# Feed-forward steps placed among attention tiles, in a two-layer audio tower on one core

## The reference

```python
ao = (gelu(concat([x, pp]) @ hop_w1 + hop_b1) @ hop_w2 + hop_b2)   # pp: phases of the positions
center, width = tanh(ao[..., :P]) * PI, sigmoid(ao[..., -1:]) * 2 + 0.1
# queries: cos/sin of center in a window of five, weighed by width; keys: tanh(x @ cpe_w) etc.
gate = sigmoid(gelu(x @ sg_w1) @ sg_w2)
st_ph = tanh(gelu(concat([x, cumsum(x @ kce_w) / pos]) @ ksk_w1) @ ksk_w2) * PI
retrieved = causal linear attention over cos/sin features, position phases and stored keys
h = h + x + layernorm(retrieved) @ out_w + out_b                   # x: layernorm(h)
f = layernorm(h)
rh = relu(f @ router_w1 + router_b1); top two of softmax(rh @ router_w2), their softmax as weights
h = h + sum over the two: w * (relu(relu(f @ w1 + b1) @ w2 + b2) @ w3 + b3)
```

## Time and profile before

| | |
|---|---|
| Three runs | 1338.63, 1339.23, 1341.33 us (median 1339.23) |
| The profiled execution | 1339.48 us, its span 1337.6 us |
| PE busy (share of span) | 1221.2 us (91%) |
| DVE | 776.2 us (58%) |
| ACT | 641.5 us (48%) |
| POOL | 527.1 us (39%) |
| Mean granted clock of PE | 0.912 |

### The profile page before, as it was taken

The page is one execution under the profiler, slowest core; times in us unless marked ns, Lnnn a source line. Parts: engine busy times, 40 slices in busy tenths (PEclk is TensorE's granted clock), DMA queues, the critical chain, the costliest instruction groups (busy, mean ns, idle before and its releaser), DMA issues.

```text
span 1337.6 us, 27027 instructions
## 1 busy us (share of the span) xinstructions
PE 1221.2 (91%) x10203; PEld 789.4 (59%) x10203; DVE 776.2 (58%) x1724; ACT 641.5 (48%) x1372; POOL 527.1 (39%) x1111
## 2 busy tenths in 40 slices
PE   6989999999999999999999997799708889889998
PEld 4755665666666666666666664545305676675553
DVE  3545555655556566565565661143677898985542
ACT  1236555555555554555555553050255664744564
POOL 3111454754554644545455444306871020421200
PEclk9979999999999999999999999799757667568999
DMA  4100000000000000000000001102110000000001
GB/s 84 18 5 2 2 3 2 4 6 2 4 2 2 3 2 2 2 2 2 3 2 3 2 2 32 62 34 48 17 14 1 1 1 1 13 1 0 13 12 23
DMA packets 34076, 14.57 MB, mean 11 GB/s; under 512 B 30738, under 2 KB 31346, under 8 KB 33949
## 3 DMA queue, kind: packets, MB, share of 16 engines
q1 hardware_dynamic: 29341, 10.95, 3.6%
q0 software_dynamic: 4608, 1.91, 1.5%
HBM read 6.46 MB, written 7.27 MB: 10 GB/s over the span
## 4 chain that ended last, share of the span: by engine, by line
PE 70%; DVE 11%; POOL 6%; issue 5%; ACT 4%; SPq 2%; DMA 1%; POOLq 0%; DVEq 0%; ACTq 0%
PE psum L755 20%; PE psum L736 10%; PE psum L664 8%; PE psum L727 7%; PE psum L711 4%; POOL XN L1311 3%; PE psum L1008 2%; PE psum L649 2%; DVE arena L1979 2%; PE psum L988 1%; PE psum L809 1%; PE psum L822 1%; PE psum L1023 1%; PE psum L688 1%; SPq L1094 1%
## 5 line engine op out<-in xcount | busy, mean ns | idle before, releaser
L1429 ACT ACTIVATE arena<-psum 125x500 f32<-125x500 f32 x576 | 307.0, 585 | 329.8 <-PE psum L736 329.8
L1780 DVE TENSOR_REDUCE arena<-psum 125x1 f32<-125x500 f32 x384 | 242.5, 674 | 199.9 <-PE psum L664 199.8
L664 PE MATMUL psum<-arena 32*125 32x500 f32 (+1 forms) x1536 | 322.4, 516 | 0.3 <-ACT arena L1420 0.3
L755 PE MATMUL psum<-arena,XN 125*64 125x250 f32 x2304 | 307.4, 387 | 0.2 <-ACT arena L1429 0.2
L736 PE MATMUL psum<-arena 32*125 32x250 f32 x2304 | 291.7, 370 | 0.0
L736 PEld LDWEIGHTS psum<-arena 32*125 32x125 f32 x2304 | 214.6, 183 | 11.8 <-issue 1.0
L755 PEld LDWEIGHTS psum<-arena,XN 125*64 125x64 f32 x2304 | 140.2, 136 | 121.2 <-issue 78.4
L1783 DVE TENSOR_REDUCE arena<-psum 125x2 f32<-125x500 f32 x192 | 121.3, 674 | 71.1 <-PE psum L664 66.9
L664 PEld LDWEIGHTS psum<-arena 32*125 32x125 f32 x1536 | 126.4, 183 | 3.7 <-DVE arena L1780 1.0
L727 PE MATMUL psum<-arena,onesb 3*125 3x500 bf16 x576 | 122.4, 422 | 2.1 <-DMA arena<-arena 2.1
L1204 POOL TENSOR_TENSOR lnst<-lnst,mhalf 125x12 f32<-125x12 f32 x14 | 32.0, 2286 | 231.3 <-DVE lnst L1759 231.3
(11 more groups left out here) (343 smaller groups left out, 1948.7 us busy)
## 6 DMA issues: line engine op xcount, KB each, us to landing
arena<-arena SPq DMA_DIRECT2D x192, 1.5 KB
expert_in<-XN SPq DMA_DIRECT2D x8, 256.0 KB, 4.8
arena<-expert_in SPq DMA_DIRECT2D x4, 512.0 KB, 5.3
expert_out<-arena SPq DMA_DIRECT2D x4, 512.0 KB, 3.1
out<-H SPq DMA_DIRECT2D x16, 93.8 KB
expert_in<-XN,slot_in POOLq DMA_INDIRECT x48
XN<-expert_out,slot_out POOLq DMA_INDIRECT x48, 3.8
arena<-in_L_ffn_w SPq DMA_DIRECT2D x2, 256.0 KB
```

What stands on the lines that cost most here:

```text
L664: last = pe.matmul(ps[0:R, at_:at_ + hi - lo], QH[row:row + 32, b, g, j * R:(j + 1) * R], KH[row:row + 32, b, g, lo:hi], start=True, stop= ...
L755: last = pe.matmul(ctx_bank[64 * h2:64 * h2 + 64, 0:THIRD], XN[:, p, c, a, :], PR[:, x % 4, h2, i * THIRD:(i + 1) * THIRD], start=(c == 0) ...
L1429: act.activation(PR[:, x % 4, h2, :], st_bank[(2 * x + h2) % 3][0:R, 0:2 * THIRD], ACT.Exp)\
L1780: dve.reduce_max(MX[:, q % 2, 0, 2 * h2 + tile:2 * h2 + tile + 1], ps[0:R, 0:2 * THIRD], AX)\
```

## The change

The list of events is written anew behind tile 7. A chain of 13 events per quarter (norm 2, product, norm 3, router, logit, weighed, gates) runs from x = 6p + 8 on at two events per x: one behind features(x), one behind the next quarters' preparation. Each x from 13 on takes one step, 28 steps in all, without a condition. Within a step the order is turned round: gate_spread of item x - 2 and layer3 come first, then layer1 of x, layer2 of x - 1, and turned a step later than before; DVE gates item x - 2.

To make room for the feed-forward's buffers beside attention's, the features are kept in two copies, HG, KG, SG, CX, RH, GP and YS in one, H2 in 6 parts instead of 12, with waits on the last reader where a copy went; late weights lie in the tiles of layer 0's Q, K and VO. POOL clears these ahead of its events, and the loads on SP follow that.

PPF and DVE's addition go; PE adds a product of the positions' phases (32 rows) to hop's product in PSUM, and ACT's Gelu reads PSUM with the bias.

Behind the list of events, the diff shows in this order: PE's `hidden` and step, POOL behind gather(3) and ahead of its events, ACT's `hidden` and step (`summed` moves ahead of `hidden1`, one step later), DVE's `gated` and step.

```diff
-        HG, at = view(0, [2 * L])
+        HG, at = view(0, [L])
...
-        CV, at = view(at, [3 * NJ, 2, 2, D], parts=R)
+        CV, at = view(at, [2 * NJ, 2, 2, D], parts=R)
...
+        qkf, vof = qkp.rearrange("p a b c -> p (a b c)"), vox.rearrange("p a b -> p (a b)")
+        e1w = qkf[:, 0:384].rearrange("p (a b) -> p a b", a=3)
...
+        H2, at = view(at, [6, HALF])
...
-        ROOM, FIRST, PER = 16, 23, 1
...
+        FIRST = 13
+        chain = [("centre", 2), ("variance", 2), ("normalize", 2), ("transpose", 2), ("product", 0), ("centre", 3),
+                 ("variance", 3), ("normalize", 3), ("transpose", 3), ("router",), ("logit",), ("weighed",), ("gates",)]
+
+        def late(x, slot):
+
+            return [(*chain[n], p) for p in range(NP) for n in (2 * (x - NJ * p - 8) + slot,) if 0 <= n < len(chain)]
+
+        todo = [("step", k) for k in range(len(steps1) + 4)]
...
             if x < NT:
                 events.append(("features", x))
+            events += late(x, 0)
             if x < NT and k in (0, 2):
...
-            if x == ROOM:
-                events.append(("room", 0))
-            for _ in range(PER if x >= FIRST else 0):
-                k = todo[0][1]
-                if x > gate_at[steps1[min(k, len(steps1) - 1)][0]] + 3:
-                    events.append(todo.pop(0))
+            events += late(x, 1)
+            if x >= FIRST and todo:
+                events.append(todo.pop(0))
...
+                        last = pe.matmul(ps[0:w.shape[1], 0:HALF], w, XT[:, cols], start=True, stop=(name == "sg"))
+                        if name == "hop":
+                            last = pe.matmul(ps[:, 0:HALF], W["hop1b"][0:PP, :], ppt[:, th * HALF:(th + 1) * HALF],
+                                             start=False, stop=True)
...
+                    if 2 <= x < len(steps1) + 2:
+                        gate_spread(x - 2)
+                    if x >= 5 and x % 3 == 2:
+                        layer3(x // 3 - 1)
                     if x < len(steps1):
                         layer1(x)
                     if 1 <= x <= len(steps1):
-                        gate_spread(x - 1)
                         layer2(x - 1)
-                    if x >= 4 and x % 3 == 1:
-                        layer3(x // 3 - 1)
-                    if x >= 5 and x % 3 == 2:
-                        turned(x // 3 - 1)
+                    if x >= 6 and x % 3 == 0:
+                        turned(x // 3 - 2)
...
+            pool.memset(b3r, 0.0)
+            pool.memset(e2w, 0.0).then_inc(S["late_zero"], 1)
+            link(pool.memset(GP, 0.0))
...
+            pool.tensor_scalar(SEL.rearrange("r p e d -> r (p e) d"), over(ramp, 6, D), 0.0, None,
+                               ALU.is_equal).then_inc(S["select"], 1)
...
-                    emptied(act, ("hop", p, th))
-                    act.activation(HG[:, own], HG[:, own], ACT.Gelu).then_inc(S["hop_act"], 1)
+                    ps, done = filled(act, ("hop", p, th))
+                    act.activation(HG[:, own], ps[:, 0:HALF], ACT.Gelu, bias=W["hopb"]).then_inc(done, 1)
...
+                    if x >= 5 and x % 3 == 2:
+                        summed(x // 3 - 1)
...
-                    if n >= 2:
-                        i = jobs[("l3", n - 2)]
+                    if n >= 1:
+                        i = jobs[("l3", n - 1)]
                         dve.wait_ge(full[i % 8], i // 8 + 1)
...
-                    if 1 <= x <= len(steps1):
-                        gated(x - 1)
-                    if x >= 5 and x % 3 == 2:
-                        added(x // 3 - 1)
+                    if 2 <= x < len(steps1) + 2:
+                        gated(x - 2)
+                    if x >= 6 and x % 3 == 0:
+                        added(x // 3 - 2)
```

More of the change, by code:

```diff
@@ L139, in build @@
         assert at <= ASIZE - 3 * 768
-        PPF = sb("PPF", [128, L])
+        ppt = sb("ppt", [PP, L])
         QH, at = view(0, [B, 2, L])
@@ L598, in _ @@
                         .then_inc(done, 1)
[L599 to L604, removed]
             for half in range(2):
@@ L866, in tokens @@
                         emptied(pe, ("ksk", p, th))
-                    pe.wait_ge(S["hop_act"], 2 * (p + 1))
+                    for th in range(2):
+                        emptied(pe, ("hop", p, th))
                 for i in range(NJ * p + 3 * h, NJ * p + 3 * h + 3):
                     cols = slice(i * R, (i + 1) * R)
-                    own = slice((i - p // 2 * 2 * NJ) * R, (i - p // 2 * 2 * NJ + 1) * R)
+                    own = slice((i - NJ * p) * R, (i - NJ * p + 1) * R)
                     ps, done = take(pe, ("tok", i))
@@ L898, in masked @@
                 p, j = divmod(x, NJ)
-                g = 2 * NJ * (p % 3) + 2 * j
+                g = 2 * NJ * (p % 2) + 2 * j
                 for k in range(2):
@@ L1326, in _ @@
             gather(3)
+            pool.memset(b3r, 0.0)
+            pool.memset(e2w, 0.0).then_inc(S["late_zero"], 1)
+            link(pool.memset(GP, 0.0))
+            for n in range(4):
+                link(pool.iota(out=ramp[32 * n:32 * n + 32, :], pattern=[[1, 6]], base=0,
+                                 channel_multiplier=-1, allow_small_or_imprecise_dtypes=True))
+            pool.tensor_scalar(SEL.rearrange("r p e d -> r (p e) d"), over(ramp, 6, D), 0.0, None,
+                               ALU.is_equal).then_inc(S["select"], 1)
             for event in events:
@@ L1337, in _ @@
                     scale(x, event[2])
-                elif kind == "room":
-                    k = jobs[("ao", NT - 1)]
-                    pool.wait_ge(full[k % 8], k // 8 + 1)
-                    pool.memset(b3r, 0.0)
-                    pool.memset(e2w, 0.0).then_inc(S["late_zero"], 1)
-                    link(pool.memset(GP, 0.0))
-                    for n in range(4):
-                        link(pool.iota(out=ramp[32 * n:32 * n + 32, :], pattern=[[1, 6]], base=0,
-                                         channel_multiplier=-1, allow_small_or_imprecise_dtypes=True))
-                    pool.tensor_scalar(SEL.rearrange("r p e d -> r (p e) d"), over(ramp, 6, D), 0.0, None,
-                                       ALU.is_equal).then_inc(S["select"], 1)
         @block.scalar
@@ L1381, in _ @@
                     last.then_inc(done, 1)
-                    for h in range(2):
-                        ps, done = filled(act, ("ppf", h))
-                        act.activation(PPF[:, h * HALF:(h + 1) * HALF], ps[:, 0:HALF], ACT.Identity, bias=W["hopb"])\
-                           .then_inc(done, 1)
             act.wait_ge(S["trig_r"], 1)
@@ L1592, in gate_tiles @@
             def gate_tiles(p):
-                if p == 0:
-                    i = jobs[("ret", 3 * NJ - 1)]
-                    act.wait_ge(full[i % 8], i // 8 + 1)
                 for th in range(2):
@@ L1617, in summed @@
                 ps, done = filled(act, ("l3", n))
-                if n >= 2:
-                    k = jobs[("yt", n - 2)]
+                if n >= 1:
+                    k = jobs[("yt", n - 1)]
                     act.wait_ge(full[k % 8], k // 8 + 1)
-                act.activation(YS[:, n % 2, :], ps[:, 0:HALF], ACT.Copy).then_inc(done, 1)
+                act.activation(YS, ps[:, 0:HALF], ACT.Copy).then_inc(done, 1)
             def hidden2(k):
@@ L1672, in _ @@
                         hidden2(x - 1)
-                    if x >= 4 and x % 3 == 1:
-                        summed(x // 3 - 1)
         @block.vector
@@ L1897, in running_mean @@
                     emptied(dve, ("xt", 1, p, h))
-                cols, own = slice(p * L, (p + 1) * L), slice(p % 2 * L, p % 2 * L + L)
-                link(dve.tensor_tensor_scan(CX[:, own], ones[:, 0:1].to_broadcast([128, L]), XT[:, cols], 0.0,
-                                            ALU.mult, ALU.add))
-                dve.tensor_tensor(CX[:, own], CX[:, own], pos1, ALU.mult).then_inc(S["cx"], 1)
-            def hop_hidden(p):
-                for th in range(2):
-                    ps, done = filled(dve, ("hop", p, th))
-                    own = slice(p % 2 * L + th * HALF, p % 2 * L + (th + 1) * HALF)
-                    dve.tensor_tensor(HG[:, own], ps[:, 0:HALF], PPF[:, th * HALF:(th + 1) * HALF], ALU.add)\
-                       .then_inc(done, 1)
+                cols = slice(p * L, (p + 1) * L)
+                if p:
+                    k = jobs[("ksk", p - 1, 1)]
+                    dve.wait_ge(full[k % 8], k // 8 + 1)
+                link(dve.tensor_tensor_scan(CX, ones[:, 0:1].to_broadcast([128, L]), XT[:, cols], 0.0,
+                                            ALU.mult, ALU.add))
+                dve.tensor_tensor(CX, CX, pos1, ALU.mult).then_inc(S["cx"], 1)
             def tokens_out(p, h):
+                if p >= 2 and h == 0:
+                    k = jobs[("ret", NJ * (p - 1) - 1)]
+                    dve.wait_ge(full[k % 8], k // 8 + 1)
```

(4 more changed lines are left out.)

121 lines of the change are left out of this document (50 added, 71 removed).

## The result

The change made the kernel slower: 1373.09 us (1371.33 to 1377.82, 4 runs) against 1339.05, ratio 1.0256 (1.0238 to 1.0275), so +34.0. The forecast was +16, with a range that reached to 1378. The profiled execution took 1377.82, its span 1376.0: 4.7 above the median, so its stretches add up to +38.4.

The account below looks back on a forecast made before the run. Among the tiles DVE, ACT and PE hand work on, with DVE nearly full; behind them PE alone bounds. Terms 1.5 + 9.5 + 16.5 + 12 - 27 + 3 = +15.5 gave 1355 us, range 1343 to 1367, far ends 1322 to 1378.

Parts of the forecast that it names:

- Tokens to chunk: From DVE's last tokens to the next quarter's first chunk: 25 us instead of 15.8, +9.2, as DVE waits for the product.
- about as much comes in by the earlier centre as goes out with hop: DVE in tiles 6 to 11: centre's added work about equals hop's removed work, making +9.2 into +9.5.
- quarter 1: Tiles 6 to 11: +9.5 us, nearly all of it between the last tokens and the next chunk.
- quarter 2: Tiles 12 to 17: +16.5 us, from +3.2 in tile 12, +3.3 in tile 13 and +10 from there on.
- Start: Up to the first tiles: +1.5 us, between -1 and +5, with 2.1 of 3.5 kept for POOL's clears.
- Quarter 3: Tiles 18 to 23: 56 us instead of 44, +12, between 2 and 25, from added steps and waits of PE.
- After tile 23: From tile 23's masked scores to the end: -27 us, between -20 and -40, as fewer steps are left.
- The latency of the norms: After the last tile: two events per tile expose the last quarter's norms, and gates wait for choices and route, +12.6 us.
- Clock: PE's granted clock: new waits of 2 to 5 us between dense steps cost +3 us, between 0 and 17.
- the tiles absorb the steps: Faster rival: DVE never waits for product or logits, tiles grow only by DVE's added work; 1332 or 1322 us, chance 0.29.
- the steps run at half clock: Slower rival: steps 0 to 10 run at half PE clock, 17 us instead of 3; 1369 or 1380 us, chance 0.14.

Follow-up runs that it names:

- e5: Changed kernel with one event per tile, norms at the places of the kernel before, and steps from x = 18: 1353.51 us, ratio 1.0115.
- e11: Kernel before with only norm 2 at two events per tile and its product early, ahead of DVE's masked scores and weights: 1359.36 us, ratio 1.0151.
- e7: Kernel before with only hop's positions moved to PE as a second pair of matmuls, without PPF and DVE's addition: 1344.80 us, ratio 1.0055.
- e2: Changed kernel with POOL's clearing and building of the late weights moved behind its first rg: 1370.26 us, ratio 1.0237.
- e1: Changed kernel with hop's positions prepared once (PPF) and added by DVE again: 1374.05 us, ratio 1.0264.
- e4: Changed kernel with steps from x = 18 instead of 13, still two events per tile: 1384.70 us, ratio 1.0349.
- e6: e5 with hop's positions on DVE again and POOL's clears behind its first rg: 1343.35 us, ratio 1.0033.
- e12: e6 with steps from x = 19 instead of 18: 1332.52 us, ratio 0.9960.

## Why the prediction was right in its mechanism and wrong in its size

- *Tokens to chunk: right.* 25 was forecast for both quarters, 26.4 and 27.3 came, with DVE waiting for the product. XT was late for two reasons at once: PE's transposes, held up by POOL, end at 1110.47, ACT's sines at 1110.58. e5 took the loss away by the pace alone, e11 made a part of it by the early norm 2 with its product.
- *The step that failed: "about as much comes in by the earlier centre as goes out with hop".* For the rest of quarter 1 that sentence put 0.3; 6.5 came (1.8 to the first tokens, 3.6 in the tokens, 1.1 behind the chunk's start). Hop's leaving gave DVE nothing, since PE was late next, by its pair: among the tiles I counted the pair in quarter 2 alone, and e7 shows 6.1 for it in the kernel before, 2.9 of them in quarter 1. The centre came in with its full 2.0, as e11 shows. In quarter 2 I put 6.5 beside the stretch; 12.4 came. 7.6 of these lie ahead of the first tokens, where DVE waits for the logits:

```profile
1155.62 0.23 DVE L2009 TENSOR_TENSOR arena<-psum,bias 125x72 f32<-125x72 f32 x1 [10.32 <-PE psum L950]
```

  PE came to them late: from 6 to 16 us behind the quarter's first features its grant was 0.53, in the kernel before 0.78, while the sum left the rise of the clock where it was and took 1.2 off for it. 3.8 lie in the tokens: 2.8 between their two halves, where the route now stands, which the sum had, and 2.3 in the second half, which ran on PE at 0.50 of the clock behind a wait for quarter 0's gates, which it had not, less 1.3 in the first half. (DVE's copy of the gates ends at 1166.12:)

```profile
1166.22 1.34 PE L963 MATMUL psum<-ident,arena 125*128 125x125 f32 x6 [1.97 <-issue]
```

  Together 12 of the 23 us that the profiled run lies above the sum; 2.9 more are the stretches themselves, 5.7 the start, 4.5 the end and 0.6 quarter 3, less the 3 put for the clock.
- *Start:* +1.5 forecast, +7.2 found (4.1 to the first features, 3.1 in tiles 0 to 5). The clears came in full, 3.5, where 2.1 was kept: DVE's gathering did not hide them (e2). Hop's pair counts in tiles 0 to 5 too (2.7 in e1, 1.6 in e7).
- *Quarter 3: right in sum.* +12 forecast, +12.6 found. The parts were not: PE was busy 53.3 us at 0.88 of the clock where 48 at full clock were forecast, and idle 4.3 where 7.5 were. That these met is luck. e4 adds what I had not seen: a step among tiles costs about half of one at the end (6.6 against 13.3 for five).
- *After tile 23:* -27 forecast, -22.5 found. The latency of the norms showed as said:

```profile
1300.08 1.48 PE L606 MATMUL psum<-ident,XN 125*128 125x125 f32 x6 [5.50 <-POOL XN L1193]
1320.34 1.48 PE L606 MATMUL psum<-ident,XN 125*128 125x125 f32 x6 [2.74 <-POOL XN L1193]
...
1339.52 0.99 PE L963 MATMUL psum<-ident,arena 125*128 125x125 f32 x6 [3.22 <-DVE arena L2047]
```

  These are 11.5 of the 12.6 forecast. But the kernel before waits there for gates too, 2.8 and 1.4, which the sum did not take off, and PE's busy time fell to 84.1 and not to 75 (114.6 less 39.8), at 0.89 of the clock instead of 0.97.
- *Clock: too small, and hidden by luck.* 3 was put for it in all. In quarter 3 and the end together PE was busy 15 us longer than the sum has it, and some 8 less idle; the second error covered half of the first.
- *Rivals.* That the tiles absorb the steps was half right of the steps (e4) and wrong of the change, since the chain of norms came with them. That the steps run at half clock gave 1369, near the time measured, and its 17 for the clock lies near the 15 above; but the grant rose to 0.74 and 0.88, so the steps did not run at half clock, and more than half of the miss (the start and quarter 1) lies ahead of any step.

The loss by parts, as far as the runs set them apart: the pace 31 us (e4 to e5), hop's pair and the clears 10 (e5 to e6); the gates' lead 11 (e6 to e12); against these, steps from 13 instead of 18 gave 12 (e4). These don't simply add up, as e1 shows. How much of any part is the clock's stays open: no run held the clock.

## What to carry to other kernels

When work is put into a software pipeline, sort it by its round trips, not by its busy time: here steps that only fill PE cost about half as much among the tiles as behind them, while a norm that goes DVE, POOL, PE, ACT, PE, DVE stalled the engine on which the next quarter's chain crosses. In this kernel such a chain did best with one event per tile and its last result ready two places or more ahead of its first reader. And the price of an edit can be cancelled elsewhere in the total (hop's pair in e1), so read it by stretch, and test it again when the larger loss is gone.

## What the runs showed of the hardware

- POOL and DVE slowed each other. POOL's scaling of a norm, begun while DVE's L1960 ran (to 1128.81), took 2.29 us instead of 1.47; DVE's next operation, begun while the scaling ran, took 1.84 instead of 0.69. L1960 itself, which had begun first, took no longer than elsewhere:

```profile
1127.86 2.29 POOL L1193 TENSOR_TENSOR XN<-XN,lnst 125x768 f32<-125x768 f32 x1
...
1128.85 1.84 DVE L1963 TENSOR_TENSOR arena<-arena 125x512 f32<-125x512 f32 x1
```

  That is 1.1 us on the chunk's chain in quarters 1 and 2. The Trainium skill ("GPSIMD Engine Reference", section "Specifications") says that GpSimd shares its SBUF interfaces with VectorE and contends with instructions of two SBUF inputs; this one has two, and the trace agrees.
- A pair of matmuls over 32 rows cost as much as one over 128: 1.61 and 1.57 us at half clock, in the changed kernel's tile 6.
- Short waits of PE in a dense stretch were followed by half the clock: 2 us for the gates among the tiles (1.00 before, 0.50 after), 2.3 in e1 (0.50 after), 2.9 to 4.3 in e6 (0.88 over 40 us, against 1.00 in e12, which lacks these waits). The Trainium skill ("TensorE: Matmul & The Clock Gate", section "Loop structure matters more than you think") says that PE goes cold when a long wait for DMA stands between every matmul; the trace agrees in kind, with single waits of these lengths, for other engines.
